# Query and key of the sparse branch from one product of 128 columns

## What is computed

```python
qkv = src @ in_proj_w.T + in_proj_b          # dense branch: 16 heads of 16
attn = softmax(q @ k.T / sqrt(dh)); ctx = attn @ v
dense_output = ctx @ out_proj_w.T + out_proj_b
Q = src @ Qp_w.T + Qp_b                      # sparse branch: Qp_w, Kp_w are 64 x 256
K = src @ Kp_w.T + Kp_b
V = src @ Vp_w.T + Vp_b
aw = softmax(Q @ K.T / sqrt(64))             # 257 x 257, the 51 largest of a row are kept
sparse_output = kept(aw) / sum(kept(aw)) @ V
fused = sig * dense_output + (1 - sig) * sparse_output
x = layernorm(src + fused)
```

## Time and profile before

| | us |
|---|---|
| timed executions | 1479.94, 1481.87, 1483.51 |
| median | 1481.87 |
| profiled execution, its own time | 1477.99 |
| its span | 1476.2 |
| outside the span | 1.8 |
| second attention, about | 598 to 1135 of the span |

### The profile page before, as it was taken

How to read it: one execution, slowest core, us unless ns; L and a number is a source line. 1 busy time by engine, 2 the same in 40 slices (tenths; PEclk the granted TensorE clock), 3 DMA queues, 4 the chain that set the end, 5 groups by cost and what they waited for, 6 DMA issues and landing times. The chain is left out here.

```text
span 1476.2 us, 21690 instructions
## 1 busy us (share of the span) xinstructions
PE 1118.4 (76%) x6799; PEld 807.9 (55%) x6799; DVE 765.7 (52%) x1788; ACT 384.5 (26%) x951; POOL 452.8 (31%) x527
## 2 busy tenths in 40 slices
PE   0358886750999990359999999999734999779888
PEld 0257774650677660235665665665422899646555
DVE  8955663230122224445556556656512377578885
ACT  0333331000222220114333334333210444222221
POOL 5941010117000007511202202211000577456665
PEclk9989998555899995667779769878657899989999
DMA  6016000102121113144314315414031200000000
GB/s 217 2 41 216 0 0 1 54 15 100 55 64 58 60 48 99 36 77 95 85 34 105 84 32 105 96 37 90 18 74 37 101 0 0 1 1 14 14 7 22
DMA packets 53403, 81.06 MB, mean 55 GB/s; under 512 B 8544, under 2 KB 45736, under 8 KB 52176
## 3 DMA queue, kind: packets, MB, share of 16 engines
q1 hardware_dynamic: 50128, 71.71, 19.1%
q0 software_dynamic: 3200, 8.43, 1.8%
HBM read 52.23 MB, written 27.62 MB: 54 GB/s over the span
## 5 line engine op out<-in xcount | busy, mean ns | idle before, releaser
L1933 DVE TENSOR_REDUCE fa_nm<-fa_ps 128x2 f32<-128x514 f32 x128 | 82.9, 690 | 74.4 <-PE fa_ps L2154 73.6
L1292 PE MATMUL ex_ps<-we_raw,ex_xT 128*128 x320 | 118.3, 494 | 0.0
L1773 ACT ACTIVATE fa_eT<-fa_ps 128x512 f32<-128x512 f32 x128 | 73.6, 590 | 81.7 <-PE fa_ps L2207 80.3
L1086 POOL DMA_INDIRECT ex_got<-y_rows,ex_pos_i x34 | 32.1, 943 | 196.9 <-DMA y_rows<-ex_y 186.8
L2945 PE MATMUL qf_ps<-qf_wg,qf_xT 128*128 128x352 f32 x272 | 89.9, 480 | 2.1 <-ACT qf_xT L2786 1.4
L2154 PE MATMUL fa_ps<-fa_ks,fa_qs 64*128 64x258 f32 x256 | 71.4, 408 | 15.4 <-DMA fa_ks<-fa_qk_rows 10.8
L447 PE MATMUL tk_ps<-tk_u,tk_qb 64*32 64x64 f32 x1024 | 22.8, 266 | 71.4 <-POOLq L314 59.7
L2207 PE MATMUL fa_ps<-fa_qs,fa_ks 66*128 66x256 f32 x256 | 71.3, 373 | 6.9 <-ACT fa_eT L1773 6.9
L1219 DVE COPY ex_hT<-ex_ps 128x384 f32<-128x384 f32 x40 | 22.3, 558 | 100.1 <-PE ex_ps L1301 100.1
L2154 PEld LDWEIGHTS fa_ps<-fa_ks,fa_qs 64*128 64x128 f32 x256 | 50.7, 258 | 40.6 <-issue 23.4
L2945 PEld LDWEIGHTS qf_ps<-qf_wg,qf_xT 128*128 128x128 f32 x272 | 50.6, 194 | 37.3 <-issue 6.6
(11 more groups left out here) (435 smaller groups left out, 2509.3 us busy)
## 6 DMA issues: line engine op xcount, KB each, us to landing
we_raw<-in_L_ffn_W SPq DMA_DIRECT2D x24, 384.0 KB
fa_qs<-fa_qk_rows SPq DMA_DIRECT2D x16, 514.0 KB
fa_ks<-fa_qk_rows SPq DMA_DIRECT2D x32, 257.0 KB, 9.9
x_rows<-tk_zero SPq DMA_DIRECT2D x1, 5120.0 KB, 19.1
ex_xin<-x_rows SPq DMA_DIRECT2D x40, 128.0 KB
y_rows<-ex_y SPq DMA_DIRECT2D x40, 128.0 KB, 1.7
fa_rsb<-fa_rs_rows SPq DMA_DIRECT2D x8, 528.0 KB
fa_qk_rows<-fa_qhl SPq DMA_DIRECT2D x32, 128.5 KB
```

What stands on the lines that cost most here:

```text
L1086: g.indirect_dma_start(out=got[0:n, a, t, :], out_offset=None, in_=y_rows[:, :], in_offset=bass.IndirectOffsetOnAxis(ap=pos_i[0:n, a, t:t ...
L1292: last = mm(ps[:, bank + t % 2, 0:HD], xT[:, t % 2, k, :], raw[:, ds(e, 1), m, k * HD:(k + 1) * HD], start=(k == 0), stop=(k == KC - 1))
L1773: cp(eT[:, j % 8, :], ps[:, ST + j % 2, :], ACT.Exp).then_inc(z["e_ready"], 1)
L1933: nc.vector.tensor_reduce(nm[:, :, j], ps[:, b:b + 2, 0:TOK], AX.X, ALU.max, negate=True).then_inc(z["max_done"], 1)
```

## The change

The two products become one with all 128 columns, written to partitions 0 to 127 of bank SB. The query then lies at partitions 0 to 63 and the key at 64 to 127. One signal is given instead of two. ScalarE's second copy reads partitions 64 to 127 and writes `k2` at 0 to 63.

```diff
             def sparse_operands(u):
-                act.wait_ge(z["q2_ps"], 2 * u + 1)
+                act.wait_ge(z["q2_ps"], u + 1)
                 cp(q2[:, :], ps[0:R, SB, 0:TOK], ACT.Identity, bias=w["bq2"][:, 0:1], scale=0.125
                    ).then_inc(z["q2_taken"], 1)
-                act.wait_ge(z["q2_ps"], 2 * u + 2)
-                cp(k2[:, :], ps[0:R, SB + 1, 0:TOK], ACT.Identity, bias=w["bq2"][:, 1:2]).then_inc(z["q2_taken"], 1)
+                cp(k2[:, :], ps[R:P, SB, 0:TOK], ACT.Identity, bias=w["bq2"][:, 1:2]).then_inc(z["q2_taken"], 1)
...
             def sparse_operands(u):
                 pe.wait_ge(z["q_taken"], KC * (u + 1))
-                for j in range(2):
-                    for k in range(KC):
-                        last = mm(ps[0:R, SB + j, 0:TOK], w["qk2"][:, k, j * R:(j + 1) * R], xT[:, k, :],
-                                  start=(k == 0), stop=(k == KC - 1))
-                    last.then_inc(z["q2_ps"], 1)
+                for k in range(KC):
+                    last = mm(ps[:, SB, 0:TOK], w["qk2"][:, k, :], xT[:, k, :], start=(k == 0), stop=(k == KC - 1))
+                last.then_inc(z["q2_ps"], 1)
```

## The result

The changed kernel is slower. Its median is 1490.04 us (22 executions, 1477.94 to 1496.73), that of the kernel before 1481.44 us (22 executions, 1475.66 to 1488.25). The ratio is 1.0050 with an interval of 1.0032 to 1.0069. The forecast was 1479.7 us, with a range up to 1484.6: wrong in sign and outside its range. The profiled execution took 1495.03 us, its span 1493.3, 17.1 us more than the span before. That is about twice the difference of the medians: the profiled execution of after is one of its long ones, and that of before (1477.99 us) was a short one.

A forecast was written before the change was run, and what follows sets the result against it. TensorE was taken as the busy engine, its savings limited by the wait for `cx`. Gains of 1.35 us, 2.2 with body 3 normal, took the median from 1481.87 to 1479.7 us; range 1475.6 or 1476 to 1484.6.

The forecast's parts named there:

- The product: L2111 in slot 3: eight records in 1.95 us become four in 1.05, saving 0.90 us a batch at full clock.
- Where a rule speaks otherwise: At L2111: by a skill rule, sparing two drains saves more than 0.90 us a batch; by the trace, nothing to spare.
- The copies on ScalarE: ScalarE's copies of q2 and k2 behind L2111: back to back, the shifted one still 0.47 us, worth 0.
- Batch 0 and body 0: Batch 0, before the ring, gains nothing; body 0, with no output projection in slot 5, gains the full 0.90 us.
- When `cx` comes: GpSimd's input to slot 5's projection: its chain starts ahead of L2111, so the change does not bring it forward.
- The stand: TensorE's wait for `cx` at slot 5's projection: grows to about 1.4 us in body 1, 1.6 in body 2, gaining 0.
- The sum: Gains over all bodies: 1.35 us on the profiled execution, 2.2 us taken for the median, giving 1479.7 us.
- Rival B: At the projection, the longer stand lowers the clock: two falls 1485.9 us, three 1489; chance 0.12 for two or more.
- Rival A: At the `cx` meeting TensorE arrives last: seven bodies gain 6.3 us, 1475.6; chance 0.33 for gains of 3 us and over.

## Why the prediction was wrong, point by point

- **The product.** Right in kind, a little small in size. Four records take 1.03 us, 1.05 was forecast. But what matters is when the work behind can start: from the start of L2111 to the start of quad 0 it was 2.32 us before (724.01 to 726.33), and after it is 1.20 (723.75 to 724.95). The saving is 1.12 us a batch instead of 0.90, and much the same in each body (1.11 to 1.12). The rest lies at the edges of the product. Its last record starts 0.31 us ahead of the next record before (725.59 and 725.90), and 0.03 us ahead of it after (724.41 and 724.43); with the two products side by side, still 64 columns wide, it is 0.31 again. Under "Where a rule speaks otherwise" the prediction found nothing to spare there; the runs show 0.2 us, in the direction of that rule. Whether it is a drain isn't shown. The pair with the class query ahead gives 1.3.
- **The copies on ScalarE.** Right: 474 to 476 ns for the shifted copy, no stand between the two, no cost.
- **Batch 0 and body 0.** Body 0, from the start of its dense products (L2103) to those of body 1, went from 53.0 to 52.5 us; 0.90 of gain was forecast. From batch 0 nothing came, as forecast.
- **When `cx` comes.** Right. It is ready 13.11, 12.77, 14.08, 13.20, 13.34 and 13.55 us after the start of the dense products in bodies 1 to 6, and was ready after 13.19, 13.53, 14.01, 12.71, 13.41 and 13.33. The change didn't bring it forward as a rule; body 2 had it 0.76 us earlier.
- **The stand.** Right in mechanism: the meeting absorbs what TensorE saves. 1.4 us was forecast for body 1, 1.39 is there. For body 2 it was 1.6, and 0.64 is there, since `cx` came early. In bodies 3 to 6 the stands are 2.52, 1.56, 1.34 and 1.32 us where about 0.9 was named, and the 0.05 to 0.30 us of gain booked there did not come. In body 3 the dense products took 5.33 us, before 6.70: TensorE came 1.4 us earlier by that and 1.1 by the change. The text named this shift of the clock as what could spoil its size.
- **The sum.** It failed as a whole: a gain of 2.2 us for the median, measured is a loss of 8.6.
- **Rival B.** This is the step that failed: not the mechanism but its chance and its place in the range. The text named it (the longer stand lowers the clock in the projection), with the price of 3.1 us a fall (measured 3.3, once 4.5) and with 1489 us for three falls. (The median is 1490.04; that this is so near is partly luck, since the 1489 include 2.2 us of gain.) But the sum has no fall in it, and the rival got 0.12, because "no stand of up to 0.71 us lowered it there". That row spoke of stands half as long as those which the same text had just forecast. Evidence from inside the old range was used for a state outside it, and the rows with a fall were weighed lower than they deserved: body 0, where a stand of 0.54 us amid short products came ahead of one, and body 7, whose projection at half clock gave the price while the 6.63 us of stand ahead of it went unread. The range, cut at one fall, left out just this case. The runs showed in its place four falls of 3.3 to 4.5 us in the profiled execution, 14.4 of 17.1 us, and the whole loss gone when the missing work was put back ahead of the wait.
- **Rival A.** It didn't come: in the profiled execution TensorE stood for `cx` in all six bodies. Why the profiled execution before was faster than the median stays open.
- **The size of 8.6 us.** At 3.3 us a fall it would be 2.6 falls an execution. The profiled execution has four, and is 17.1 us longer by span; the other executions have no trace, but their mean granted clock lies between 0.820 and 0.835, with the fastest at 0.835 and the profiled one at 0.822. So a fall isn't certain in a body, and an execution varies with their number. That is inferred, not shown; shown is that with the work ahead of the wait no body fell and the 8 us were gone.
- **The rest of the 17.1 us.** Bodies 0 to 5, from L2103 to L2103, differ by -0.5, +2.7, +0.4, +4.8, +6.3 and +3.3 us; body 6, from L2103 to the projection of body 7, by -0.3. The falls make 3.3, 4.5, 3.3 and 3.3 of those in bodies 1, 3, 4 and 5. What is left is mostly body 4, 3.0 us, and not a matter of the projection: body 4 of the kernel before was an unusually short one, 51.36 us with a mean clock of 0.87, where bodies 1, 2, 3 and 5 had 0.77 to 0.81 and body 4 of after has 0.77. Body 3 had a late transfer in both kernels (2.36 us from `rs_out` to `rsb` in after; the earlier trace rows have 2.40 in body 3 and 1.46 in body 4); before, TensorE arrived just as late, after it stood 2.52 us.

What the rows of after tell of the fall itself: after quad 0 TensorE has two short records (0.50 us), stands, and within 0.5 us of the projection's start the clock is at 0.50, in body 3 already in the stand. In other kernels it came up to 2.0 us behind the start. Why 1.32 us in body 6 did nothing and 1.34 in body 5 did stays open, and with it what exactly decides on a fall; shown is that the lost work ahead of the wait brings the falls about. The rule "A second HAM failure mode: psum-queue depth-cycling" of the Trainium skill, page "TensorE: Matmul & The Clock Gate", which the prediction cited, says that micro-idles between groups of matmuls make the clock swing. At the projection of bodies 1 to 6 the trace of after bears it out where that of before didn't: the idles are 1.3 to 2.5 us long in five bodies instead of 0 to 0.7, and there are four falls.

## What to carry to other kernels

Time saved on TensorE ahead of a wait that something else sets is not just lost: it turns into a longer stand with less work ahead of it, and the dense work behind the wait can then run at half clock. Before taking work off TensorE, look for the next meeting, write down how long its stand will be, and price a fall of the clock on the work behind it; that no shorter stand has lowered it is no argument. Where it does fall, move useful work ahead of the wait, or keep the old work there, and look at the meeting after it, which may take the gain again. And move it only where there is a stand to fill: in the kernel before, with next to none, the same move of the class query cost 0.8%.

## What the runs showed of the hardware that was not expected

- Two products of 64 columns, written to partitions 0 to 63 and 64 to 127, run side by side: eight records in 1.10 us, against 1.95 when both write to partitions 0 to 63.
- Once down, the clock stayed at 0.50 for 6.8 us in three of the falls of after and for 10.2 us in that of body 3, nearly all of it with TensorE busy; the price was 3.3 and 4.5 us of projection. The stretches of those of bodies 1 and 3:

```profile
728.87:735.70 6.83, 6.83 (x17) 4.55 (x16) 4.11 (x14) 0.00 (x0) 0.93 (x1) 0.50 1.10 206
841.51:851.75 10.24, 9.33 (x20) 6.04 (x20) 5.26 (x17) 0.00 (x0) 1.70 (x3) 0.50 0.93 173
```

- 0.60 us of dense records directly ahead of stands of 1.55 and 1.56 us went without a fall, and that kernel's median shows no loss (1481.3 us). The reverse, more dense records in the stage but behind the wait, didn't help: 1492.76 us.
- A product of 64 columns has a dearer end than one of 128: its last record starts 0.31 us ahead of the next record, that of the 128 columns 0.03 us, both ahead of the same turned scores.
- The executions of after differ more among themselves: they range over 1.3% (1477.94 to 1496.73), those of before over 0.9%, with 22 executions each.
